# A two-layer image kernel with a hand-written step plan: an earlier load slot, steps that run on over a sample's end, and bf16 products left out

## The reference

```
...
x = x + conv(gn(x))
...
xz = u @ W_in.T;  xs, z = split(xz)
xc = silu(conv1d(xs) + conv_b)
dt, Bm, Cm = split(xc @ W_x.T)
delta = softplus(dt @ W_dt.T + b_dt)
h_t = exp(delta * A) * h_(t-1) + delta * Bm * xc
y = (sum over the 16 states of h * Cm) + xc * D
x = x + (y * silu(z)) @ W_out.T
```

## Time and profile before

| | before |
|---|---|
| median of 3 runs | 6219.44 us (6212.93 to 6222.01) |
| the profiled execution's own time | 6214.45 us |
| its span, first to last instruction | 6212.4 us |
| mean granted TensorE clock | 0.957 of full speed |
| busy share of the span | PE 94%, DVE 90%, POOL 84%, ACT 81% |
| stretch of samples 0 to 13 in the trace | 326.6 to 5517.2 us, about 370.8 us a sample |

### The profile page before, as it was taken

How to read it: one execution, slowest core, us unless ns; L and a number is a source line. 1 busy time by engine, 2 the same in 40 slices (tenths; PEclk the granted TensorE clock), 3 DMA queues, 4 the chain that set the end, 5 groups by cost and what they waited for, 6 DMA issues and landing times. The chain is left out here.

```text
span 6212.4 us, 98864 instructions
## 1 busy us (share of the span) xinstructions
PE 5847.0 (94%) x31168; PEld 2967.3 (48%) x31168; DVE 5581.0 (90%) x5483; ACT 5062.2 (81%) x8658; POOL 5204.6 (84%) x5092
## 2 busy tenths in 40 slices
PE   8999999999999999999999999999999999998776
PEld 5645445454454545455454554545444454544222
DVE  0089999999999999999899998999999999999999
ACT  5588888888888888888888888888888888887765
POOL 0078889898898988889898898988888898899998
PEclk9999999999999999999999999999999999998765
DMA  3367776777767767676677766667676676767663
GB/s 96 95 166 169 165 164 161 168 163 172 168 154 165 163 170 168 160 172 161 160 171 170 165 162 161 163 168 169 161 176 154 159 175 163 169 146 167 132 142 76
DMA packets 803005, 980.09 MB, mean 158 GB/s; under 512 B 388686, under 2 KB 414970, under 8 KB 802490
## 3 DMA queue, kind: packets, MB, share of 16 engines
q1 hardware_dynamic: 802490, 973.77, 66.9%
HBM read 716.13 MB, written 257.43 MB: 157 GB/s over the span
## 5 line engine op out<-in xcount | busy, mean ns | idle before, releaser
L1230 POOL TENSOR_TENSOR hc<-hs,cs 128x512 f32<-128x512 f32 x3072 | 3834.6, 1272 | 579.0 <-DVE hs L1189 354.8
L1189 DVE TENSOR_TENSOR_SCAN hs<-av,state,b 128x512 f32<-128x512 f32 x2688 | 3247.1, 1260 | 2.5
L1053 ACT ACTIVATE av<-rep_d,nega 128x512 f32<-128x512 f32 x3072 | 2106.7, 714 | 25.5 <-DVE hs L1189 19.7
L1179 DVE TENSOR_TENSOR b<-rep_u,pb 128x1024 f32<-128x1024 f32 x1024 | 1241.7, 1213 | 129.0 <-PE pb L888 123.5
L897 PE MATMUL py<-hc,rsel 128*32 128x512 f32 x6144 | 1139.7, 633 | 69.5 <-POOL hc L1230 63.6
L810 PE MATMUL cb<-xu,w1a 96*128 96x388 f32 (+1 forms) x2400 | 925.6, 498 | 23.5 <-ACT xu L993 8.0
L815 PEld LDWEIGHTS cb<-w2c,g 128*97 128x97 f32 x9408 | 851.8, 166 | 153.7 <-issue 111.7
L815 PE MATMUL cb<-w2c,g 128*97 128x96 f32 x9408 | 887.7, 251 | 6.7 <-ACT rr L993 6.7
L852 PE MATMUL cb<-xn,wtap 96*96 96x512 f32 x1536 | 743.1, 621 | 2.6 <-ACT xn L1074 2.6
L1001 ACT ACTIVATE g<-cb,b1a 128x388 f32<-128x388 f32 (+1 forms) x1200 | 660.5, 568 | 70.3 <-PE cb L810 59.7
L1182 DVE TENSOR_TENSOR b<-rep_u,pb 128x512 f32<-128x512 f32 x1024 | 700.8, 684 | 0.0
(11 more groups left out here) (110 smaller groups left out, 6555.8 us busy)
## 6 DMA issues: line engine op xcount, KB each, us to landing
rep_d<-delta_scratch SPq DMA_DIRECT2D x512, 384.0 KB, 7.0
rep_u<-deltax_scratch SPq DMA_DIRECT2D x512, 384.0 KB, 6.8
cs<-c_scratch SPq DMA_DIRECT2D x512, 256.0 KB, 6.6
delta_scratch<-dlt SPq DMA_DIRECT2D x128, 384.0 KB, 3.7
deltax_scratch<-dlt SPq DMA_DIRECT2D x128, 384.0 KB, 7.7
v_scratch<-v2s SPq DMA_DIRECT2D x192, 192.0 KB
t1r<-t_scratch SPq DMA_DIRECT2D x144, 240.0 KB, 5.2
xb<-in_x SPq DMA_DIRECT2D x128, 192.0 KB, 4.4
```

What stands on the lines that cost most here:

```text
L1053: act.activation(av[:, n % NAV, :], rep_d[:, k % 2, j, :], ACT.Exp, scale=nega[:, q, j:j + 1])\
L1179: dve.tensor_tensor(b3[:, 0:2, :], rep_u[:, k % 2, 3 * hf:3 * hf + 2, :], pb[:, None, :].broadcast_to([128, 2, T]), ALU.mult).then_inc(dve ...
L1189: dve.tensor_tensor_scan(hs[:, n % NHS, :], av[:, n % NAV, :], b3[:, n % 3, :], start, ALU.mult, ALU.add)\
L1230: pool.tensor_tensor(hc[:, n % NHC, :], hs[:, n % NHS, :], cs[:, k % 2, g % NQ, :], ALU.mult)\
```

## The change

The change has four parts. `WLD_AT` puts WLD at slot 71: one slot after the slot of `W_up` 24, and not before slot 64. `padded` puts the PAD step at slot 150 (or at the plan's last slot, if that is earlier) and sorts it in. `plan_of` no longer adds the WARM rows. And `iteration` no longer takes all rows that are left at the end of a sample: it keeps them in `late` with their slot less 192, and takes them in the next sample at that slot, ahead of that sample's own rows; only the plan ahead of the loop and the last one still take them at their end.

```diff
+PAD_AT = 150
...
-        rows += [(W_LAST + 1, ("WLD", 0)), (W_FIRST + 1, ("WG", 0))] + [r for r in W_ROWS if r[0] < NC8 * NU]
+        rows += [(WLD_AT, ("WLD", 0)), (W_FIRST + 1, ("WG", 0))] + [r for r in W_ROWS if r[0] < NC8 * NU]
...
 def padded(rows):
-    rows = sorted(rows, key=lambda r: r[0])
     n = sum(st[0] not in UNRINGED for _, st in rows)
-    return rows + [(rows[-1][0], ("PAD", i)) for i in range(-n % RING)]
+    pads = [(min(PAD_AT + 3 * i, max(p for p, _ in rows)), ("PAD", i)) for i in range(-n % RING)]
+    return sorted(rows + pads, key=lambda r: r[0])
...
-    return padded(rows + (warm(rows) if kind != "tail" else []))
+    return padded(rows)
...
+WLD_AT = max(S_LAST + 4, 1 + next(p for p, st in W_ROWS if st == ("W_up", NB - 1)) - NC8 * NU)
...
-            def iteration(st, chunks, units, last=False):
+            late = []
+
+            def iteration(st, chunks, units, last=False, carried=True):
                 todo = list(st.plan)
...
+                        while late and late[0][0] <= k * NU + n:
+                            step_fn(*late.pop(0)[1:])
                         while todo and when(todo[0]) <= k * NU + n:
                             step_fn(st, todo.pop(0)[1])
-                for _, step in todo:
-                    step_fn(st, step)
+                assert not late
+                late.extend((when(row) - NC8 * NU, st, row[1]) for row in todo)
+                while late and not carried:
+                    step_fn(*late.pop(0)[1:])
...
-            iteration(Steps(BEFORE[3], starts[3], starts[3] // RING, -1, BEFORE[2]), (NC8 - 2, NC8 - 1), False)
+            iteration(Steps(BEFORE[3], starts[3], starts[3] // RING, -1, BEFORE[2]), (NC8 - 2, NC8 - 1), False, carried=False)
...
-            iteration(Steps(LAST, base, base // RING, NS - 1, TAIL), range(NC8 + 1), True, last=True)
+            iteration(Steps(LAST, base, base // RING, NS - 1, TAIL), range(NC8 + 1), True, last=True, carried=False)
```

## The result

The changed kernel takes 6074.61 us (median of 4 runs, 6072.77 to 6076.34) against 6218.54 us before: a ratio of 0.9769, 95% interval 0.9752 to 0.9786, or 143.9 us less. The forecast was 6030 us, 188 us less. The profiled execution took 6074.4 us, its span is 6072.6 us, and the mean granted clock 0.958 (0.957 before).

The account below looks back on a forecast made before the run. DVE's own work was taken as the bound, its idle time as the gain: 9.8 (load) + 2.7 (sample's end) + 0.9 (products, PAD) = 13.4 us a sample, 14 times 188 us, giving 6030 us; range 5978 to 6100.

Parts of the forecast that it names:

- The sum's own bounds: Whole change, adding the parts' bounds: 10.8 to 17.2 us a sample, 151 to 241 us in all, 6068 to 5978 us.
- the rival in which the clock falls: PE's clock falls once in each sample and DVE pays all 5.1 us: 8.3 us a sample gained, 6103 us; chance 0.10.
- The earlier load: Slots 82 to 87: WLD at slot 71 ends the `t1r` wait; gain 9.8 us a sample, bounds 9.0 and 11.7.
- The sample's end: Rows run into the next sample: 3.88 us wait goes, 1.2 us comes at its start; gain 2.7 us, bounds 2.0 and 3.88.
- the sum over two groups only: After the sample's end, new `pb` waits counted only at slot 3 (0.8 us) and the next group (0.4 us).
- The products and PAD: 317 PE products left out, PAD moved to slot 150: gain 0.9 us a sample, bounds -0.25 and 1.6.
- That ends this wait and leaves PE about as late as before in the next groups: Slots 147 to 153: 0.82 us of products less, 0.25 us of PAD more, ends DVE's 0.63 us wait at 153.
- The clock: PE's clock in full samples without products: expected to hold mostly, though groups at slots 15 and 39 are 1.1 and 1.6 us lighter.
- the first rival: PE's clock falls once a sample, as in sample 14, and DVE pays all 5.1 us: 6103 us; chance 0.10.
- a sign that it is wrong: Clock at 0.5 in other places of a full sample with DVE waiting for `pb` there, or PE waiting for `rr` or `xt`.
- The sentence that no row shows such a fall: On the skill's rule that an idling PE is throttled: the trace agrees for sample 14, no row shows it for full samples.
- The other rivals: D's loads late, 6103 us (0.06); no new waits, 5978 (0.10); load still late, 6170 (0.02); slower, PE bound, 6318 (0.04).

## Why the prediction was right or wrong

The sign, the bounding engine and the range held; the size was 44 us too large. The sum's own bounds, 6068 to 5978 us, do not hold the 6074.61 us; the range does, because it was drawn out to 6100 for the rival in which the clock falls. Step by step, with the parts measured alone:

| part | predicted, us a sample | measured, us a sample |
|---|---|---|
| load at slot 71 | 9.8 (9.0 to 11.7) | 10.0 (139.7 / 14) |
| rows over the end, with all products | 2.7 (2.0 to 3.9) | 0.9 (12.8 / 14) |
| products left out, by putting them back | 0.9 (-0.25 to 1.6) | -0.6 (-8.0 / 14) |
| whole change | 13.4 | 10.3 (143.9 / 14) |

The third column spreads the whole difference over 14 samples. By the profiled executions the samples 1 to 13 became 10.7 us shorter each and sample 0 5.4, while sample 14 became 4.3 longer; and leaving the products out made the samples 1 to 13 0.2 us shorter each, and sample 0 8.2 us longer.

- **The earlier load: right, in its size too.** 7.6 us of PE's work between two `pb` was forecast and 7.66 measured; 1.9 us were to stay at slot 87 and 1.63 did. D's first steps wait for no transfer, as costed.
- **The sample's end: mechanism right, size wrong while the products stand.** The wait at slot 3 was forecast at 0.8 us and is 0.77; the one at slot 6 (0.4) does not come. The step that failed is the sum over two groups only: without the pause PE stays behind for longer, and the rest comes back at slots 15 and 27. With the products out, the waits at 3, 15 and 27 are 1.56 us, 0.2 of which was there before, so in the changed kernel the part would be worth up to 2.5. It may be less: the wait at 39 is 0.46 us with the products alone left out and 1.46 in the changed kernel. No run has this part without products and with WLD at its old slot.
- **The products and PAD: next to nothing where a gain was forecast.** "That ends this wait and leaves PE about as late as before in the next groups" is the step that failed. It took PE for late at slot 152 in any case. PE was late there because of the products: without them it comes 2.4 us earlier (the three at 147 account for 0.7 of this) and idles for an input that comes when POOL makes it. The wait at 153 went, as forecast; in its place came 2 us of idle time, a clock fall and 3.1 to 4.7 us at 156. That eats what is won at the other slots. PAD at 150 was costed at 0.25 us; it costs 0.3 there and saves 0.3 at slot 3.
- **The clock: the first rival came, in part.** "I expect the clock to hold mostly" was wrong: all 14 samples have at least one fall, with DVE waiting behind it, which the prediction had named as a sign that it is wrong. The price was also too high: a fall here costs DVE 1.7 us, not 5.1, because it is the shorter kind (at 1.2 GHz for 3.4 us, not 10.2); X's late start costs another 1.4 us at 156 and 0.3 at 159, and both together make the 3.4 to 3.6 us by which an undisturbed sample is longer than with DG2 moved (358.2 against 354.6). So the time fell between the forecast and that rival's 6103. The sentence that no row shows such a fall in a sample of this load was wrong already for the kernel before: its trace has one at slots 84 to 86 of each of the samples 1 to 13, in sample 5 during the 7.85 us of idle time of the earlier trace rows. The rule of the Trainium skill ("TensorE: Matmul & The Clock Gate", "HAM oscillation — how this bites in real kernels"), that a PE which idles between bursts begins the next one at half rate, is drawn there from waits for a DMA, longer than the 2.27 us here. The changed kernel's trace agrees with it in kind: the clock falls at X behind that idle time in every sample. The run without products alone does not: the same 2 us, three falls in 13 samples. The prediction read the rule as advice to keep the products. All 22 put back give 6066.6 us; the reason to idle removed, which is what arranging the work means here, gives 6017.4.
- **The other rivals** did not come. PE waits neither for `t1r` nor for D's `rr` and `xt`, and it is not the bound.

Left open: why the changed kernel falls at slot 153 in every sample, while the kernel before without products, with the same 2 us of idle time, does so in three of 13. There the samples last 367.7 to 373.1 us, here nine of 14 last 358.2; whether that matters was not tried. Open too is why the clock falls at 44 and 164 in some samples and not in others.

## What to carry to other kernels

A filler on a nearly full engine is neither free nor useless: it can pay where the engine would idle ahead of heavy work, and it costs up to its own time where the engine is behind. Before it is taken out, look for what the engine will wait for when it comes earlier, along the chain through the other engines; that wait, not the filler, is the thing to mend (here one step moved by two slots, worth 57 us). And when a pause of the bounding engine is removed, follow the engine behind it for a whole chunk, not for two groups, since the pause was also its time to catch up.

## What the runs showed of the hardware

- PE's clock fell behind idle times of about 2 us within otherwise busy groups: 2.27 us before X in all 14 samples of the changed kernel, 1.96 us in 13 of 14 with PAD at 191, but 1.97 us in three of 13 with the products alone left out. After 1.53 us it stayed up in all samples of two runs with three products at 147 and fell in one sample of a third.
- It fell too at slot 44, where PE was not idle: in the changed kernel with DG2 moved, no idle time above 0.2 us stands in the slots 36 to 44 before the fall of sample 6. Every run without the products at 39 has such falls in some samples; with three of them back there is none.
- A fall of 10.2 us at slot 44 cost DVE 3.5 of the 5 us that PE lost. A fall of 3.4 us, 1.7 us of PE's time, cost DVE nearly all of it near slots 68, 153 and 164 (1.5 to 1.7 us), and 0.2 us at slot 44.
- The tail sample (14), whose own plan is the same, went from 345.6 to 349.9 us. The late rows of sample 13 now run into it (0.77 us of wait at slot 3), and one of its falls came at slot 53 in place of 42 (2.93 us of wait at slot 57, none before). Where single falls decide, a change elsewhere can shift them.
